# Graph attention on one core: the transposes of x ahead of a column of products, the relu ahead of the copies, in the first row group

## What is computed

```python
h = jnp.maximum(_layernorm(x, axis=-1), 0.0)
Wh = h @ W
f1 = Wh @ a1
f2 = Wh @ a2
e = jax.nn.leaky_relu(f1[:, None] + f2[None, :], negative_slope=0.2)
e = jnp.where(adj == 0, -jnp.inf, e)
attention = jax.nn.softmax(e, axis=1)
x = x + attention @ Wh
```

## Time and profile before

| | us |
|---|---|
| median of 3 runs (810.04 to 810.56) | 810.08 |
| the profiled execution | 810.9 |
| its span | 809.2 |
| TensorE busy | 785.9 |
| VectorE busy | 740.8 |
| ScalarE busy | 483.5 |
| GpSimd busy | 419.2 |

### The profile page before, as it was taken

The page is one execution under the profiler, slowest core; times in us unless marked ns, Lnnn a source line. Parts: engine busy times, 40 slices in busy tenths (PEclk is TensorE's granted clock), DMA queues, the critical chain, the costliest instruction groups (busy, mean ns, idle before and its releaser), DMA issues.

```text
span 809.2 us, 22590 instructions
## 1 busy us (share of the span) xinstructions
PE 785.9 (97%) x8969; PEld 718.5 (89%) x8969; DVE 740.8 (92%) x1189; ACT 483.5 (60%) x777; POOL 419.2 (52%) x621
## 2 busy tenths in 40 slices
PE   5899999999999999999999999999999999999997
PEld 4778799999999999999999999999999999999986
DVE  6997899999999999999999999999999999999996
ACT  6788865655655565565555556565555656555542
POOL 7687755544545554454545445454544545454320
PEclk9999999999999999999999999999999999999999
DMA  9998899999999999999999999999999999998200
GB/s 172 169 106 85 79 108 114 110 96 107 85 101 95 97 91 88 110 85 101 91 100 91 87 110 86 101 88 104 90 88 107 89 100 86 106 90 87 27 14 17
DMA packets 48321, 75.99 MB, mean 94 GB/s; under 512 B 4768, under 2 KB 13600, under 8 KB 48288
## 3 DMA queue, kind: packets, MB, share of 16 engines
q0 software_dynamic: 43008, 67.13, 87.8%
q1 hardware_dynamic: 4864, 8.39, 3.1%
q10 hardware_dynamic: 416, 0.07, 0.0%
HBM read 272.70 MB, written 4.19 MB: 342 GB/s over the span
## 4 chain that ended last, share of the span: by engine, by line
PE 90%; issue 3%; ACT 2%; DVE 2%; POOL 2%; DMA 1%; ACTq 0%; POOLq 0%; DVEq 0%
PE acc L392 53%; PE acc L396 27%; PE stage L382 7%; PE stage L365 2%; DVE wt_ring L811 1%; PE stage L373 1%; ACT ht L542 1%; DMA a_sb<-in_L_gnn_a_dram 1%; PE stage L349 1%; POOL xn L248 0%; ACT wh L549 0%; POOL tmp L267 0%; POOL masks L224 0%; POOL masks L239 0%; ACT tmp L562 0%
## 5 line engine op out<-in xcount | busy, mean ns | idle before, releaser
L811 DVE SCALAR_TENSOR_TENSOR wt_ring<-stage,packed,marks 128x512 f32<-128x512 f32 x1024 | 697.6, 743 | 54.1 <-PE acc L396 42.5
L392 PE MATMUL acc<-pairs,wt_ring 128*128 128x258 f16 x4096 | 718.9, 274 | 2.4 <-DVE pairs L801 1.3
L396 PE MATMUL acc<-pairs,wt_ring 128*128 128x129 f16 x4096 | 697.4, 219 | 0.0
L392 PEld LDWEIGHTS acc<-pairs,wt_ring 128*128 128x128 f16 x4096 | 396.0, 97 | 56.7 <-DVE pairs L801 2.2
L571 ACT ACTIVATE marks<-stage 128x1024 uint16<-128x1024 uint8 x256 | 262.0, 1023 | 290.5 <-PE stage L382 289.3
L396 PEld LDWEIGHTS acc<-pairs,wt_ring 128*128 128x128 f16 x4096 | 399.5, 98 | 2.5
L239 POOL TENSOR_TENSOR masks<-masks 128x256 int32<-128x256 int32 x256 | 184.2, 734 | 240.4 <-ACT masks L591 239.6
L214 POOL DMA_DIRECT2D masks<-in_adj_dram x240 | 130.3, 545 | 99.5 <-PE stage L382 77.5
L591 ACT ACTIVATE masks<-masks 128x512 uint16<-128x512 uint16 x256 | 158.9, 622 | 0.5 <-DMA masks<-in_adj_dram 0.5
L382 PE MATMUL stage<-ident,masks 128*128 128x128 f32 x512 | 99.2, 276 | 1.5 <-POOL masks L239 0.9
L382 PEld LDWEIGHTS stage<-ident,masks 128*128 128x128 f32 x512 | 53.0, 141 | 6.4 <-issue 2.8
(11 more groups left out here) (60 smaller groups left out, 143.9 us busy)
## 6 DMA issues: line engine op xcount, KB each, us to landing
masks<-in_adj_dram POOLq DMA_DIRECT2D x256, 256.0 KB, 7.4
out_dram<-xm SPq DMA_DIRECT2D x15, 256.0 KB, 7.2
xm<-in_x_dram SPq DMA_DIRECT2D x1, 1536.0 KB, 13.4
xm<-in_x_dram SPq DMA_DIRECT2D x1, 1024.0 KB, 10.5
xm<-in_x_dram SPq DMA_DIRECT2D x1, 768.0 KB, 5.8
xm<-in_x_dram SPq DMA_DIRECT2D x1, 512.0 KB, 7.6
xm<-in_x_dram SPq DMA_DIRECT2D x1, 256.0 KB, 3.2
out_dram<-xm SPq DMA_DIRECT2D x4, 64.0 KB, 2.6
```

What stands on the lines that cost most here:

```text
L392: return nc.tensor.matmul(acc[:, r, 0:2 * E1], wtv[:, w, r, 1, :], pairv[:, t, :, 0:E1], start=st, stop=end)
L396: return nc.tensor.matmul(acc[:, r, 0:E1], wtv[:, w, r, 0, :], pairv[:, t, 0, 0:E1], start=False, stop=False)
L811: nc.vector.scalar_tensor_tensor(out=wtq[:, t % NW], in0=e_row, scalar=packed[:, t, 1:2], in1=edges[:, k], op0=ALU.max, op1=ALU.mult).then ...
```

## The change

On TensorE x_transposes(b+3) goes from behind the products k=1 to in front of them, right behind features(b+2, 0). On ScalarE relu(b+3) goes from behind unpack(b+2) to right behind `second`, ahead of root, keep(b+2, 1), exponentials(b+2) and unpack(b+2).

```diff
@@ TensorE, first row group, for k in range(PACK)
                         product(b, r, k)
                     if b + 2 < NQ and k == 0:
                         features(b + 2, 0)
-                    if b + 3 < NQ and k == 1:
+                    if b + 3 < NQ and k == 0:
                         x_transposes(b + 3)
                     if b + 2 < NQ and k == 1:
                         features(b + 2, 1)
@@ ScalarE, first row group, for b in range(UN)
                 for u in SECONDS.get(b, (b + 3,)):
                     second(u // UN, u % UN)
+                if b + 3 < NQ:
+                    relu(b + 3)
                 if b in ROOTS:
                     root(ROOTS[b])
                 if b + 2 < NQ:
...
                     exponentials(b + 2)
                 if b + 2 < UN:
                     unpack(b + 2, b + 2, first=True)
-                if b + 3 < NQ:
-                    relu(b + 3)
                 if b + 4 < NQ:
                     normalise(b + 4)
```

## The result

The changed kernel takes 813.77 us (median of 5 runs, 813.70 to 814.82) against 810.56 us (5 runs, 810.04 to 810.75): ratio 1.0046, 95% interval 1.0033 to 1.0059. It is slower by 3.2 us, and 3.1 were forecast. The profiled execution took 813.77 us with a span of 812.1, 2.9 more than before.

What follows compares the result with a forecast made beforehand. Bound: a loop through ScalarE's relu, 4.77 us a block. Early blocks (+0.85) and nine GpSimd loops of 5.23 us give +3.6, block 13 -0.5: net +3.1, 813.2 us; range 810.8 to 817.0, the forecast's own 812.0 to 814.3.

Steps and rivals of the forecast that it cites:

- Two loops, the longer one rules: First row group: a loop through ScalarE's relu, 4.77 us a block, rules; one through GpSimd's scaled and normalise, 4.56, is hidden.
- The transposes' move puts the 0.67 us of k=1 into GpSimd's loop: On TensorE, transposes ahead of k=1 bring its 0.67 us into the loop through GpSimd, 4.56 becoming 5.23 us a block.
- The relu's move costs nothing: On ScalarE, the earlier relu costs nothing and covers 0.65 us; alone worth up to 4.77 us down to the next loop.
- 5.23 us a block: Length of the loop through GpSimd after the change, between bounds 5.15 and 5.33; nine such loops from block 3 to 12.
- 0.35 us that GpSimd was early: In block 9, normalise() on GpSimd ends at 68.45 us, 0.35 us before the transposes needing it start at 68.80.
- The early blocks: Up to block 3, features(5, 1) starts at 40.2 us instead of 39.35, +0.85, with block 1 at low clock.
- Rival B: Blocks 1 and 3 come earlier as VectorE's inverses may precede GpSimd's scaled: +1.4 us, 811.5 us, no measurable change; chance 0.14.
- Block 13 gives back 0.5: Block 13 has no transposes and loses its wait for relu: about 3.85 us instead of 4.34, -0.5.
- Rival A: GpSimd's true results land before their recorded ends, so its chain isn't late: -2.8 us, 807.3 us; chance 0.10.
- Rival C: VectorE's low part meets GpSimd's scaled() in every block, 0.26 us each, +2.3: 815.5 us; chance 0.08.
- Rival D: TensorE's idle pieces bring low clock in half of nine blocks, about 1.2 us each, +5.4: 818.6 us; chance 0.06.
- The hand-over of the loss to the end one for one: What row group 1 loses reaches the end one for one, unless a later wait swallows it: net +3.1 us.

Runs made afterwards that it cites:

- experiment 5: The kernel before, with only GpSimd's order changed: normalise(b+4) before scaled(b+2); 811.12 us against 810.43, ratio 1.0009.
- (3): The changed kernel with GpSimd doing normalise(b+4) before scaled(b+2); 808.64 us, ratio 0.9978 to the kernel before.
- experiment 1: The changed kernel with the transposes put back behind column k=1, so only the relu goes ahead; 809.67 us against 810.44 for the kernel before, ratio 0.9989.
- experiment 2: The kernel before with only the transposes moved ahead of column k=1, the relu staying behind the unpack; 814.44 us, ratio 1.0051.
- 7: The changed kernel with transposes behind k=1 and normalise before scaled on GpSimd except in blocks 0, 2 and 6; 809.87 us, ratio 0.9995 to the kernel before.
- 8: The changed kernel with normalise before scaled, and root and inverses heading their engines' lists in blocks 0, 2, 6; 809.47 us, ratio 0.9984 to the kernel before.
- experiment 9: The changed kernel with only root and inverses at the head of their lists in blocks 0, 2 and 6; 815.75 us, ratio 1.0060 to the kernel before.

## Why the prediction was right, point by point

- *Two loops, the longer one rules.* Right. Cutting GpSimd's gained nothing in the kernel before (experiment 5) and turned the changed kernel from a loss into a gain (3); cutting ScalarE's alone gave blocks of 4.59 us (1).
- *The transposes' move puts the 0.67 us of k=1 into GpSimd's loop.* Right: alone it costs 4.0 us (2; the nine blocks of its profile take 47.51 us against 44.29), and the block is 5.27 us with or without the relu's move, 4.59 with the transposes back, a difference of 0.68.
- *The relu's move costs nothing.* Right; together with the old place of the transposes it is 0.8 us faster. "Up to the next loop" was too hopeful: in the one profile the nine blocks won 1.48 us, and a stretch of low clock in block 3 took 1.0 of it (1). The copy behind relu did not wait longer, as the prediction's list of signs had it, but 0.57 us instead of 0.65, with another 0.46 before relu.
- *5.23 us a block.* Measured 5.27 to 5.28. The semaphore from GpSimd to TensorE took 0.10 us, not 0.14; features to copy took 0.70, not 0.65, when products and not the transposes stand before it; transposes and k=1 took 1.14, not 1.11. The prediction's 0.35 us that GpSimd was early contains the semaphore: by its own sums the slack was 4.77 - 4.56 = 0.21 us. Nine blocks made +3.17 over before; +2.8 was forecast.
- *The early blocks.* The term of the sum that was mis-sized: +0.85 forecast, +0.14 measured, although features(2, 0) started 0.66 us later in this execution (19.80 against 19.14). Most of it is one step: the transposes and k=1 of block 1 were put in at low clock, 0.85 + 1.29 = 2.14 us, as in the trace before. In the profile after, that place ran at full clock and took 1.14:

```profile
27.24 0.63 PE L349 MATMUL stage<-ident,xn 128*128 128x128 f32 x4 [0.74 <-issue]
...
28.38 0.66 PE L365 MATMUL stage<-wx,ht 128*128 128x130 f32 x4
```

  The table of stretches says it directly, the kernel before first (0.50), the profile after second (1.00):

```profile
26.00:29.00 3.00, 3.00 (x19) 2.68 (x18) 3.00 (x7) 1.18 (x3) 2.13 (x4) 0.50 1.12 241
```

```profile
26.00:29.00 3.00, 2.26 (x23) 2.01 (x22) 3.00 (x7) 2.04 (x5) 2.65 (x5) 1.00 1.12 243
```

  The low clock was there after the change too, but in block 0 (0.50 from 20.5 to 23.5 us), and the waits of 0.77 and 1.08 us that TensorE has right behind that time in the kernel before (ending at 23.75 and 25.67) are not there. So -1.00 for the clock and -0.04 for the semaphore, +0.52 because normalise(4) ended at 27.14 and not at 26.62, and -0.19 in blocks 2 and 3: -0.71. With the low clock in block 1 the term came out near its size (experiment 2). The stretch lies in block 0, 1, 2 or 3, or nowhere, from one profile to the next, and no run tries whether the edit moves it.

  Rival B's mechanism did happen too, in block 0. VectorE in the profile after:

```profile
23.00 0.17 DVE L768 TENSOR_TENSOR small<-small 128x8 f32<-128x8 f32 x1
23.20 0.17 DVE L769 SCALAR_TENSOR_TENSOR small<-small 128x8 f32<-128x8 f32 x1
...
24.75 0.17 DVE L792 TENSOR_SCALAR packed<-stage 128x8 f16<-128x8 f32 x1 [0.90 <-ACT tmp L562]
```

  scaled() started at 24.79 us, after the inverses were through; normalise then began at 25.83 without waiting for them. How much of that comes from the relu's place and how much from the late start and the low clock of block 0 is not separated. In block 2 the meeting stayed (L769 took 1.06 us).
- *Block 13 gives back 0.5.* 0.43.
- *Rival A* (GpSimd's recorded ends are too late) falls: twelve transposes waited, and began 0.10 us after the recorded end. *Rival C*: in this kernel scaled() kept 1.05 us in blocks 4 to 12, so the low part did not lie over it; it did in experiment 1, where blocks are shorter. The low part met GpSimd's mix instead in blocks 7, 8, 11 and 12 (1.07 to 1.09 us), and these kept 5.27 us. *Rival D*: the granted clock was 1.00 from 36 to 94 us although TensorE stood still 0.45 to 0.74 us before the transposes of each block.
- *The hand-over of the loss to the end one for one*: +3.09 us at block 15, +2.9 in the span, +3.2 in the medians.

The errors of two terms, -0.7 in the early blocks and +0.4 in the loop, partly cancelled, and the last low part, 0.90 instead of 0.69 us, added 0.2. That the total is within 0.1 us is luck beyond the 0.5 or so that the terms deserve, and so is the block 15 product at 97.19 where 97.2 was forecast.

## What to carry to other kernels

Where engines pass work round in a loop, write down every loop through the edited place, the ones that show no wait too, with the slack of each: here the hidden loop was 0.2 us from ruling, and a move that put 0.67 us into it cost more than cutting the ruling one won. Move an operation early only as far as its slowest input allows, and if the input is behind something unrelated in its engine's list (scaled() here), swap those first: the same change lost 3.2 us or won 2.5 by that order alone. The name beside an idle time is not the proof of a cause; take the loop's term out and see whether the period shrinks by it. And a time read in a stretch of low clock is not a term of the kernel: look at the granted clock of the row before taking it over, for in the next execution the stretch may lie elsewhere.

## What the runs showed of the hardware

Who starts first, VectorE or GpSimd, decided up to a microsecond at a time. The low part took 0.69 us alone and 1.43 when it started 0.18 us behind scaled(); the inverses' instructions took 0.17 us or 0.92 to 1.06. The Trainium skill, SBUF — State Buffer, section Who interferes with whom, says that a VectorE instruction with two SBUF inputs contends with a GpSimd instruction that reads SBUF, and that the order of issue decides who blocks. These rows agree: the low part and the inverses have two such inputs; the low part that came second ended 0.55 us after scaled(), an instruction of the inverses 0.03. The runs of one kernel spread: the relu alone over 3.2 us in 11 runs, the kernel before over 1.9 in 27. Whether the meetings make this spread, or the place of the low clock below, was not tested.

TensorE's granted clock was 1.00, its level of 2.4 GHz, from 4 to 124 us in five of the eleven profiles. In the other six it was 0.50, the level of 1.2 GHz, for one stretch of 3.4 us: from 20.2 us in the changed kernel, 25.9 in the kernel before, 38.2 in experiment 1, 26.1 in 2, 31.9 in 7 and 19.9 in 8. It moved k=1 and the transposes from 1.1 to 2.1 us where it fell on them. TensorE had stood still before it, in the kernel before 0.77 and 1.08 us, in experiment 1 1.17 and 1.51. But experiment 9's kernel stood still 1.45, 1.13 and 1.22 us and kept 1.00, so such waits alone did not decide it. The busy time of the early blocks doesn't tell either; the changed kernel first, experiment 9's second:

```profile
18.00:42.00 24.00, 20.46 (x191) 18.23 (x190) 22.26 (x58) 19.60 (x43) 16.01 (x24) 0.93 1.18 174
```

```profile
18.00:42.00 24.00, 17.60 (x170) 15.26 (x170) 22.54 (x54) 17.36 (x42) 16.55 (x23) 1.00 1.19 171
```

The busier of the two had the lower clock, though the low clock itself lengthens the busy time. Of what set it off the runs show nothing more.
